# A sorted expert stage in 24 groups instead of 31, sixteen of them of two halves

## The chip, the core and the metric

The kernel runs on one core of one Trainium2 chip. The time is that of the device, in microseconds (us), for one execution of the whole program. A core has five engines with a queue each: TensorE (PE in the profile, with its weight loads as PEld), VectorE (DVE), ScalarE (ACT), GpSimd (POOL) and SyncE (SP), which here only issues DMAs. Engines wait for each other by semaphores. SBUF is the working memory, of 128 partitions; TensorE writes into PSUM.

## The reference, cut to what matters

A decoder layer on 2048 tokens of width 256: a linear recurrence, a cross attention, and a feed-forward part with one shared expert and 16 routed ones, of which each token uses one (K = 1). The change is in the feed-forward part:

```
logits = hidden @ router_w.T
top_vals, top_idx = jax.lax.top_k(logits, K)              # K = 1 of N = 16
scores = sigmoid(top_vals at top_idx, -inf elsewhere)
routed_in = hidden[None, :, :] * scores.T[:, :, None]
gate_up = jnp.einsum('nth,nhf->ntf', routed_in, gate_up_proj)
gate, up = jnp.split(gate_up, 2, axis=-1)
routed_out = jnp.einsum('ntf,nfh->nth', up * silu(gate), down_proj)
shared = silu(hidden @ shared_gate_w.T) * (hidden @ shared_up_w.T) @ shared_down_w.T
x = _layernorm(x + shared + routed_out.sum(axis=0))
```

H and F are 256, the shared width 1024. Everything is float32.

## The kernel before

The program has the stages `before_attention`, `attention`, `route_and_share` and `experts`, each a block in which every engine has its own written-out list of work; a block ends with a barrier of all engines. The change touches the last two.

**Routing and the shared expert** (`route_and_share`). Tokens lie in 16 tiles of 128. The shared expert runs in four chunks of 512 tokens; a chunk has eight steps of hidden columns (`gate_up` on TensorE, `gates` on ScalarE, `hidden` on VectorE), then four tiles of `down`, to which VectorE adds the layer's input in place (`residual`, into `x2`, semaphore `v_base`). While chunk 0 ends, VectorE finds each token's expert (`choose`), and from the counts of two matmuls (`count`) the place of each token in a sorted list (`place`): expert by expert, each expert's rows start at a multiple of 128. The worst case needs 16 + 15 = 31 tiles (`ETILES`). `experts()` of that stage makes the table `te`: tile j belongs to expert te[j]. GpSimd scales each row by its score (`x2s`, eight tiles at a time) and scatters it, with its token number as a 257th column, to `sorted_x` in DRAM by an indirect DMA (line 1068). SyncE had filled `sorted_x` with zeros and the number 2048 (no token) before, and stores the sum of input and shared expert in token order in `routed` (`store_base`, line 1013).

**Experts** (`experts`). One tile j of 128 sorted rows after the other, in a ring of eight:

- SyncE loads `xs` (sorted rows), eight tiles ahead;
- TensorE transposes it (`transpose_x`, L1554), ScalarE copies it to SBUF (L1456), TensorE multiplies by the gate and up weights of expert te[j] (`gate_up`, L1560, 128 x 512 into `bgu`);
- ScalarE makes the silu (L1460), VectorE the product (L1491), TensorE transposes it (`transpose_h`, L1569), VectorE copies (`copy_h`, L1495), TensorE multiplies by the down weights (`down`, L1578, 128 x 256 into `by`);
- VectorE adds the residual row `base` (`whole`, L1507), takes its statistics (L1509, L1512); GpSimd makes the inverse deviation of two tiles at a time (`inverse`, L1419 and L1421), VectorE the shift (L1517), ScalarE normalises (L1465);
- GpSimd gathers `base` from `routed` by the row numbers, two tiles ahead (L1412), and scatters the result to `out` (L1426); rows with number 2048 are skipped.

TensorE's order in slot j is `transpose_x(j+1)`, `transpose_h(j-1)`, `gate_up(j)`, `down(j-1)`; GpSimd's in step j is `gather(j+2)`, with odd j `inverse`, then `store(j-3)`. VectorE's is `copy_h(j-1)`, `product(j)`, `row_number(j+1)`, with odd j `shift`, `whole(j-1)`. The engines run eight slots written out, then hardware loops (`Fori`) of eight, then the rest.

Of the kernel before, what the change touches and what calls it, by code (L numbers as in the profile page):

```python
# [5 lines left out]
F32 = mybir.dt.float32  # L6
# [6 lines left out]
P = 128  # L13
# [882 lines left out]
ETILES = TILES + EXPERTS - 1  # L896
# [7 lines left out]
def route_and_share(nc, io, mem):  # L904
# [9 lines left out]
    with ExitStack() as ctx:  # L914
# [26 lines left out]
        incl = sb("incl", [P, EXPERTS])  # L941
        off = sb("off", [P, 2, EXPERTS])
        posf = sb("posf", [P, TILES])
        cmpj = sb("cmpj", [P, ETILES, EXPERTS])
        tef = sb("tef", [P, 2, ETILES])
# [15 lines left out]
        d_r, d_wd, d_zero, d_scatter = sem("d_r"), sem("d_wd"), sem("d_zero"), sem("d_scatter")  # L961
        g_zero = sem("g_zero")
# [23 lines left out]
        def _(sp):  # L986
# [23 lines left out]

            def store_base(c):
                sp.wait_ge(v_base, (c + 1) * QT)
                sp.dma_start(io["routed"][0:S, :].rearrange("(t p) n -> p t n", p=P)[:, c * QT:(c + 1) * QT, :],
                             x2[:, c * QT:(c + 1) * QT]).then_inc(mem["d_base"], 16)

            for c in range(CHUNKS - 1):
                store_base(c)
# [8 lines left out]
            store_base(CHUNKS - 1)  # L1026

        @block.gpsimd
        def _(pool):
# [21 lines left out]
            for half in range(2):  # L1051
# [59 lines left out]
        def _(dve):  # L1111
# [38 lines left out]

            def place():

                counts = carry[:, TILES, :].unsqueeze(2).to_broadcast([P, EXPERTS, TILES])
                thresholds = grid[:, GRID_THR:GRID_THR + TILES].unsqueeze(1).to_broadcast([P, EXPERTS, TILES])
                step(dve.tensor_tensor(work[:, 0], counts, thresholds, ALU.is_gt))
                step(dve.tensor_reduce(nt[:], work[:, 0], AX.X, ALU.add))
                step(dve.tensor_tensor_scan(incl[:], onesr[:], nt[:], 0.0, ALU.mult, ALU.add))
                step(dve.tensor_tensor(off[:, 0], incl[:], nt[:], ALU.subtract))
                step(dve.tensor_scalar(off[:, 1], off[:, 0], float(P), None, ALU.mult))
                step(dve.tensor_tensor(work[:, 0], bp[:, 0:256].rearrange("p (t n) -> p t n", n=EXPERTS),  # L1160
                                       carry[:, 0:TILES, :], ALU.add))
                step(dve.tensor_tensor(work[:, 1], work[:, 0], by_expert(off[:, 1]), ALU.add))
                step(dve.tensor_tensor(work[:, 0], work[:, 1], oneh[:], ALU.mult))
                step(dve.tensor_reduce(posf[:], work[:, 0], AX.X, ALU.add))
                dve.tensor_copy(pos[:], posf[:]).then_inc(v_pos, 1)

            def experts():

                tiles = grid[:, GRID_J:GRID_J + ETILES].unsqueeze(2).to_broadcast([P, ETILES, EXPERTS])
                step(dve.tensor_tensor(cmpj[:], by_expert(incl[:], ETILES), tiles, ALU.is_le))  # L1170
                step(dve.tensor_reduce(tef[:, 0], cmpj[:], AX.X, ALU.add))
                step(dve.tensor_scalar(tef[:, 1], tef[:, 0], float(EXPERTS - 1), None, ALU.min))
                step(dve.tensor_copy(te[:], tef[:, 1]))
# [54 lines left out]
            count()  # L1228
            place()
            residual(0, (2, 3))  # L1230
            experts()
            with dve.Fori(1, CHUNKS) as c:
                for f in range(FK):
                    hidden(c, f)
                residual(c)
# [93 lines left out]
TURNS = (ETILES - 1) // UNROLL  # L1329

def experts(nc, io, mem):

    te, ident = mem["te"], mem["ident"]
    w_gate_up, w_down = mem["w_gate_up"], mem["w_down"]
    with ExitStack() as ctx:  # L1336
# [30 lines left out]
        g_c4, filler = sem("g_c4"), sem("filler")  # L1367
# [5 lines left out]

        block = ctx.enter_context(nc.Block())

        @block.sync
        def _(sp):
            xs_rows = io["sorted_x"].rearrange("(t p) n -> p t n", p=P)

            def load(j, r):  # L1380
                sp.dma_start(xs[:, r], xs_rows[:, bass.ds(j, 1), :].squeeze(1)).then_inc(d_xs[r], 16)

            with sp.Fori(0, TURNS - 1) as i:
                for r in range(UNROLL):
                    sp.wait_ge(p_x, i * UNROLL + (r + 1))
                    sp.wait_ge(v_row, i * UNROLL + (r + 1))
                    sp.sem_inc(filler, 1)
                    load(i * UNROLL + (r + UNROLL), r)
            for j in range(TURNS * UNROLL, ETILES):
                sp.wait_ge(p_x, j - UNROLL + 1)  # L1390
                sp.wait_ge(v_row, j - UNROLL + 1)
                load(j, j % UNROLL)
            for r in range(UNROLL):
                sp.wait_ge(d_y[r], 16 * ((ETILES - 1 - r) // UNROLL + 1))

        @block.gpsimd
        def _(pool):
# [8 lines left out]
            def gather(j, r, reused):  # L1406
                pool.wait_ge(v_row, j + 1)
                pool.sem_inc(filler, 1)
                if reused:
                    pool.wait_ge(v_y, j - AHEAD + 1)  # L1410
                    pool.sem_inc(filler, 1)
                pool.indirect_dma_start(base[:, r % AHEAD, :], None, io["routed"][0:S, :], bass.IndirectOffsetOnAxis(row[:, r:r + 1], 0),  # L1412
                                        bounds_check=S - 1, oob_is_err=False).then_inc(d_b[r % AHEAD], 16)

            def inverse(m, r, n):

                pair = slice(r, r + n)
                pool.wait_ge(v_mv4, 2 * m + n)
                pool.tensor_tensor(ve4[:, pair], mv4[:, pair, 1], eps4[:, 0:n], ALU.add).then_inc(g_l4, 1)  # L1419
                pool.wait_ge(g_l4, m + 1)  # L1420
                pool.tensor_tensor(rstd4[:, pair], ve4[:, pair], mhalf4[:, 0:n], ALU.pow).then_inc(g_r4, 1)  # L1421

            def store(j, r):
                pool.wait_ge(a_out, j + 1)
                pool.sem_inc(filler, 1)
# [3 lines left out]
            def step(j, n, m):  # L1429

                if not (isinstance(j, int) and j + 2 >= ETILES):
                    gather(j + 2, (n + 2) % UNROLL, not (isinstance(j, int) and j + 2 < AHEAD))
                if n % 2:
                    inverse(m, n - 1, 2)
                if not (isinstance(j, int) and j < 3):
                    store(j - 3, (n - 3) % UNROLL)

            gather(0, 0, False)
            gather(1, 1, False)
            for n in range(UNROLL):  # L1440
                step(n, n, n // 2)
# [252 lines left out]
```

## Time and profile before

| what | us |
|---|---|
| median of 3 runs (lowest, highest) | 941.9 (939.98, 943.53) |
| the profiled execution, its own time | 938.92 |
| its span in the trace | 937.1 |
| PE busy in the span | 891.1 (95%) |
| stage `experts`: first instruction to the end of the span | 820.99 to 937.1 |
| the last `gate_up` of the stage starts | 917.80 |
| the last scatter to `out` starts and ends on GpSimd | 930.75, 931.77 |
| busy in the stretch 826 to 917.8: PE, DVE, ACT, POOL | 90.70, 52.02, 34.09, 67.21 |

The profiled execution is 3.0 us under the median; 1.8 us of its time lie outside its span. A matmul's end in the trace is modelled, and matmuls overlap: the distance from one start to the next says what one costs, not its duration. A busy PE says that something is in its array, not that nothing could be left out.

### The profile page before, as it was taken

To read this page: it belongs to the slowest core of one execution; us is meant where nothing else is said; L and a number is where in the kernel's file an instruction comes from. 1 tells how busy PE (TensorE), PEld (TensorE's weight loads), DVE (VectorE), ACT (ScalarE), POOL (GpSimd) and SP (SyncE) were. 2 spreads that over 40 slices of the span, in tenths; PEclk is the share of its full clock that TensorE was granted. 3 is DMA by queue.
4 is the path that set the end of the run, shared out by engine and by line. 5 is a ranking of instruction groups with operands and counts; after the bars stand their busy time and mean duration, and the time that the engine had idled before them with its cause. 6 is when DMAs were issued, how large, how long until landed. Compare 5 with 4: busy or idle time off the path is not lost. (4 is left out here: it accounts for less than half of the span.)

```text
span 937.1 us, 12963 instructions
## 1 busy us (share of the span) xinstructions
PE 891.1 (95%) x4616; PEld 527.6 (56%) x4616; DVE 551.5 (59%) x1123; ACT 351.8 (38%) x493; POOL 593.3 (63%) x397
## 2 busy tenths in 40 slices
PE   6998799999999999999999999998899999989993
PEld 3655355545555555565554564544678888855551
DVE  2898557667747767757766756754645121145552
ACT  2245144434525544435443434451441121123332
POOL 0454198898878889869889869882114400047785
PEclk9999899999999999999999999999999999999997
DMA  8013300000001000001000001040795100423210
GB/s 277 27 50 111 109 1 1 23 1 1 1 1 45 24 1 1 1 1 46 23 1 0 2 1 45 1 157 1 197 351 193 54 14 22 135 90 111 81 39 15
DMA packets 42873, 52.86 MB, mean 56 GB/s; under 512 B 4400, under 2 KB 33856, under 8 KB 42816
## 3 DMA queue, kind: packets, MB, share of 16 engines
q1 hardware_dynamic: 35808, 44.21, 14.8%
q0 software_dynamic: 3744, 6.32, 2.1%
q10 hardware_dynamic: 3264, 1.57, 0.6%
q8 instruction: 36, 0.59, 0.3%
q14 instruction: 21, 0.17, 0.1%
HBM read 38.42 MB, written 17.59 MB: 60 GB/s over the span
## 5 line engine op out<-in xcount | busy, mean ns | idle before, releaser
L607 POOL TENSOR_TENSOR accG<-accG,probs 128x1024 f32<-128x1024 f32 (+1 forms) x170 | 405.2, 2384 | 38.5 <-ACT probs L630 23.4
L630 ACT ACTIVATE probs<-st 128x1024 f32<-128x1024 f32 (+1 forms) x208 | 212.7, 1026 | 202.9 <-PE st L794 197.3
L674 DVE TENSOR_REDUCE mxp<-mx 128x1 f32<-128x512 f32 x360 | 231.9, 686 | 60.0 <-PE mx L780 54.6
L816 PE MATMUL av<-probs,V 128*64 128x512 f32 (+1 forms) x832 | 191.7, 598 | 0.0
L780 PE MATMUL mx<-K_hi,Q_hi 64*128 64x512 f32 (+1 forms) x480 | 137.9, 380 | 0.0
L816 PEld LDWEIGHTS av<-probs,V 128*64 128x64 f32 (+1 forms) x832 | 55.4, 136 | 105.7 <-issue 83.9
L794 PE MATMUL st<-Q_hi,K_hi 64*128 64x512 f32 (+1 forms) x416 | 113.0, 445 | 0.9 <-ACT probs L630 0.9
L780 PEld LDWEIGHTS mx<-K_hi,Q_hi 64*128 64x128 f32 x480 | 73.8, 184 | 52.0 <-issue 26.8
L794 PE MATMUL st<-M,ones_r 64*128 64x512 f32 (+1 forms) x416 | 101.1, 392 | 0.0
L794 PE MATMUL st<-Q_hi,K_lo 64*128 64x512 f32 (+1 forms) x416 | 96.7, 392 | 0.0
L794 PE MATMUL st<-Q_lo,K_hi 64*128 64x512 f32 (+1 forms) x416 | 94.5, 394 | 0.0
L794 PEld LDWEIGHTS st<-Q_hi,K_hi 64*128 64x128 f32 (+1 forms) x416 | 48.3, 180 | 47.0 <-ACT probs L630 30.5
L689 DVE RECIPROCAL misc<-misc 128x128 f32<-128x128 f32 x64 | 61.4, 960 | 13.5 <-PE misc L833 13.5
L1560 PE MATMUL bgu<-w_gate_up,xsT 128*128 x124 | 58.4, 594 | 1.0 <-ACT xsT L1456 1.0
L1177 DVE TENSOR_TENSOR hT<-hT,bu 128x512 f32<-128x512 f32 x32 | 22.0, 687 | 61.8 <-ACT hT L1090 57.5
L1295 PE MATMUL bt<-wd,hT 128*128 128x256 f32 x256 | 56.3, 380 | 0.4 <-DVE x L1186 0.4
L1090 ACT ACTIVATE hT<-bg 128x512 f32<-128x512 f32 x32 | 19.1, 597 | 99.4 <-PE bu L1280 97.2
L607 POOL TENSOR_TENSOR accG<-probs 128x1024 f32<-128x1024 f32 x16 | 38.3, 2395 | 27.9 <-ACT probs L630 27.9
L794 PEld LDWEIGHTS st<-M,ones_r 64*128 64x128 f32 (+1 forms) x416 | 50.9, 181 | 7.2 <-DVE M L659 0.3
L1295 PEld LDWEIGHTS bt<-wd,hT 128*128 128x128 f32 x256 | 48.5, 190 | 7.4 <-DVE x L1186 0.8
L1398 POOL MEMSET mhalf<- 128x2 f32 x1 | 0.1, 99 | 82.9 <-POOLq L914 82.9
L794 PEld LDWEIGHTS st<-Q_lo,K_hi 64*128 64x128 f32 (+1 forms) x416 | 49.6, 182 | 3.7
(198 smaller groups left out, 1238.0 us busy)
## 6 DMA issues: line engine op xcount, KB each, us to landing
w_gate_up<-in_gate_up SPq DMA_DIRECT2D x4, 2048.0 KB, 20.1
w_down<-in_down SPq DMA_DIRECT2D x2, 2048.0 KB, 15.8
xs<-scratch_sorted_x SPq DMA_DIRECT2D x31, 128.5 KB
scratch_sorted_x<-zero SPq DMA_DIRECT2D x7, 514.0 KB, 8.3
xT<-in_xT SPq DMA_DIRECT2D x4, 512.0 KB, 6.7
xring<-in_x SPq DMA_DIRECT2D x4, 512.0 KB, 8.7
scratch_x1b<-xT SPq DMA_DIRECT2D x4, 512.0 KB, 2.9
x<-scratch_x1b SPq DMA_DIRECT2D x4, 512.0 KB, 4.3
```

The costliest lines, as they stand in the source:

```text
L607: pool.tensor_tensor(total[0:r], so_far[0:r], probs[0:r, place(S, t)], ALU.add).then_inc(g_add, 1)
L630: act.activation(probs[0:r, place(S, t)], st[g % 2][0:r, :], ACT.Exp, scale=DH ** -0.5).then_inc(a_probs, 1)
L674: dve.tensor_reduce(mxp[:, F % 2, h * QT + i, j:j + 1], mx[h][:, 0:kn], AX.X, ALU.max).then_inc(v_mx, 1)
L689: dve.reciprocal(misc[:, cols], misc[:, cols]).then_inc(v_rsum, 1)
L780: mm = pe.matmul(mx[h][:, a * kn:(a + 1) * kn], Q_hi[F % 2][rows, q * P:(q + 1) * P], K_hi[rows, F % PAIRS, k0:k0 + kn], start=True, stop= ...
L794: mm = pe.matmul(st[g % 2][0:r, h * QC:(h + 1) * QC], w, q, start=(part == 0), stop=(part == MAXIMA))
L816: mm = pe.matmul(av[h * DH:(h + 1) * DH, :], V[0:r, t, (2 * p + h) * DH:(2 * p + h + 1) * DH], probs[0:r, place(S, t), h * QC:(h + 1) * QC ...
L1090: act.activation(hT[:, f], bg[f % 2][:], ACT.Silu).then_inc(a_silu, 1)
L1177: dve.tensor_tensor(hT[:, f], hT[:, f], bu[f % 2][:], ALU.mult).then_inc(v_h, 1)
L1295: mm = pe.matmul(bt[i % 2][:, 0:D], hT[:, f, i * P:(i + 1) * P], wd[:, f, :], start=(f == 0), stop=(f == FK - 1))
L1398: pool.memset(mhalf4[:], -0.5).then_inc(g_c4, 1)
L1560: mm = pe.matmul(bgu[r % 2][:], xsT[:, r, k * P:(k + 1) * P], w_gate_up[:, bass.ds(e * DK + k, 1), :].squeeze(1), start=(k == 0), stop=(k ...
```

## The change

The sorted list gets another layout of 24 groups of 128 rows. An expert with n rows fills ceil(n/128) - 1 whole tiles first ("pairs" in the code: two halves of 64); these go to groups 0 to 7, of which each has one expert, from `te` (`WHOLE` = 8). The remaining 1 to 128 rows of expert e are its rest: the first 64 of them go to the second half of group 8 + e, whose expert is fixed; rows past 64 of a rest ("odd") go to the first half of one of the groups 8 to 23, with an expert from `te`. If whole tiles are more than eight, the further ones take first halves too (`over`, `BEYOND`, `spread`). So groups 8 to 23 are computed with two experts' weights: each matmul with 128 columns of stationary rows becomes two with 64, which write to the PSUM partitions 0 to 63 and 64 to 127 (`products`). All 24 groups are always computed.

The residual rows are sorted too. In place of `store_base` and of GpSimd's gathers, GpSimd scatters each finished tile of `x2` to a second DRAM list `sorted_base` (`scratch_base`), twelve tiles in the routing stage and four at the start of the expert stage; SyncE fills that list with zeros before, and in the expert stage loads `base` with plain DMAs, four groups ahead, after `d_base` has counted all 16 scatters. The loops of the expert stage are written out for 24 groups, `te` is read once per slot instead of twice, and GpSimd's order becomes `store`, `store`, `inverse`. ScalarE normalises two groups together. VectorE's routing work grows and is put between the steps of the shared expert's chunk 1.

```diff
-ETILES = TILES + EXPERTS - 1
+HALF = P // 2
+WHOLE = TILES // 2
+ETILES = WHOLE + EXPERTS
...
-            for c in range(CHUNKS - 1):
-                store_base(c)
+            for t in range(0, ETILES, ZT):
+                n = min(ZT, ETILES - t)
+                sp.dma_start(mem["sorted_base"].rearrange("(t p) n -> p t n", p=P)[:, t:t + n, :],
+                             zero[:, 0:D].unsqueeze(1).to_broadcast([P, n, D])
+                             ).then_inc(d_bzero, 16)
...
-            store_base(CHUNKS - 1)
...
+            pool.wait_ge(d_bzero, 16 * ((ETILES + ZT - 1) // ZT))
+            for t in range(TILES - QT):
+                pool.wait_ge(v_base, t + 1)
+                pool.indirect_dma_start(mem["sorted_base"][:, :], bass.IndirectOffsetOnAxis(pos[:, t:t + 1], 0),
+                                        x2[:, t], None).then_inc(mem["d_base"], 16)
...
             count()
+            per_expert()
+            residual(0, (2, 3))
+            hidden(1, 0)
+            offsets()
+            hidden(1, 1)
+            past_pairs()
+            hidden(1, 2)
             place()
-            residual(0, (2, 3))
+            hidden(1, 3)
+            spread()
+            hidden(1, 4)
+            experts_at()
+            hidden(1, 5)
             experts()
...
+            def load_base(j):
+                at_least(sp, v_y, j - AHEAD + 1)
+                sp.dma_start(base[:, j % AHEAD], base_rows[:, j, :]).then_inc(d_b[j % AHEAD], 16)
+
+            sp.wait_ge(mem["d_base"], 16 * TILES)
+            for j in range(AHEAD):
+                load_base(j)
+            for j in range(UNROLL, ETILES + AHEAD):
+                if j < ETILES:
+                    load(j)
+                load_base(j - AHEAD)
...
-            pool.memset(base[:, :, :], 0.0).then_inc(g_c4, 1)
-            pool.wait_ge(g_c4, 3)
-            pool.wait_ge(mem["d_base"], 16 * CHUNKS)
...
+            for tile in range(TILES - QT, TILES):
+                pool.indirect_dma_start(mem["sorted_base"][:, :], bass.IndirectOffsetOnAxis(pos[:, tile:tile + 1], 0),
+                                        x2[:, tile], None).then_inc(mem["d_base"], 16)
...
+            inverse(0)
+            for m in range(1, ETILES // 2):
+                store(2 * m - 2)
+                store(2 * m - 1)
+                inverse(m)
+            store(ETILES - 2)
+            store(ETILES - 1)
...
+            def products(out, cols, rows_T, j, chosen, weights):
+
+                for k in range(DK):
+                    chosen_rows = weights[:, bass.ds(chosen * DK + k, 1), :].squeeze(1)
+                    if j < WHOLE:
+                        mm = pe.matmul(out[:, 0:cols], rows_T[:, k * P:(k + 1) * P], chosen_rows, start=(k == 0), stop=(k == DK - 1))
+                    else:
+                        own = (j - WHOLE) * DK + k
+                        pe.matmul(out[0:HALF, 0:cols], rows_T[:, k * P:k * P + HALF], chosen_rows, start=(k == 0), stop=(k == DK - 1))
+                        mm = pe.matmul(out[HALF:P, 0:cols], rows_T[:, k * P + HALF:(k + 1) * P], weights[:, own, :],
+                                       start=(k == 0), stop=(k == DK - 1))
+                return mm
```

**TensorE, one slot of the expert stage.** Before, from the second `gate_up` matmul (k = 1) of a tile to the first `down` matmul of the tile before it; ISA and TENSOR_LOAD rows are register work and the read of `te`:

```order
L1560 ISA
L1560 MATMUL bgu<-w_gate_up,xsT 128x512
L1547 TENSOR_LOAD te
L1547 ISA x2
L1578 ISA [waits v_y,v_hT]
L1578 MATMUL by<-w_down,hTt 128x256
```

The same piece of a slot of the groups 8 to 23 in the changed kernel:

```order
L1598 ISA
L1598 MATMUL bgu<-w_gate_up,xsT 64x512
L1599 MATMUL bgu<-w_gate_up,xsT 64x512
L1598 ISA [waits v_y,v_hT]
L1598 MATMUL by<-w_down,hTt 64x256
L1599 MATMUL by<-w_down,hTt 64x256
```

Each matmul of 128 rows has become two of 64 with the same number of streamed columns, and the second read of the table is gone. The transposes around this piece stay at 128 x 128.

**GpSimd, the start of the expert stage.** Before, from the stage's first instruction (L1412 gathers residual rows, L1419 and L1421 are `inverse`, L1426 scatters the output):

```order
L1398 MEMSET mhalf 128x2
L1400 MEMSET eps 128x2 [waits g_c4]
L1402 MEMSET base 128x1024 [waits g_c4]
L1412 DMA base<-scratch_routed,row 128x256 [waits v_row,g_c4,d_base]
L1412 DMA base<-scratch_routed,row 128x256 [waits v_row] x3
L1419 TENSOR_TENSOR ve<-mv,eps 128x2 [waits v_mv4]
L1421 TENSOR_TENSOR rstd<-ve,mhalf 128x2 [waits g_l4]
L1412 DMA base<-scratch_routed,row 128x256 [waits v_row,v_y] x2
```

The changed kernel, from the same place (L1486 scatters the last four residual tiles, L1500 the output):

```order
L1481 MEMSET mhalf 128x2
L1483 MEMSET eps 128x2 [waits g_c4]
L1486 DMA scratch_base<-x_49,pos 3072x256 [waits g_c4]
L1486 DMA scratch_base<-x_49,pos 3072x256 x3
L1493 TENSOR_TENSOR ve<-mv,eps 128x2 [waits v_mv4]
L1495 TENSOR_TENSOR rstd<-ve,mhalf 128x2 [waits g_l4]
L1500 DMA out<-ysb,row 2048x256 [waits a_out] x2
```

The gathers are gone, four scatters stand before everything else, and two output scatters stand between one `inverse` and the next.

**VectorE, from the counts to the shared expert's chunk 1.** In the changed kernel (L1239 is `hidden`, L1248 `residual`; the tables `per_...` and `off_...`, one number per expert, are new):

```order
L1170 TENSOR_TENSOR over<-over 128x1 [waits v_route]
L1171 TENSOR_SCALAR per_odd_to<-per_odd_to,over 128x16 [waits v_route]
L1248 TENSOR_TENSOR x_49<-bt,x_49 128x256 [waits p_dn,g_x2s,v_route]
L1248 TENSOR_TENSOR x_49<-bt,x_49 128x256 [waits p_dn]
L1239 TENSOR_TENSOR hT<-hT,bu 128x512 [waits a_silu]
L1175 TENSOR_TENSOR off_pair<-per_pairs_to,per_pairs 128x16
L1176 TENSOR_SCALAR off_pair<-off_pair 128x16 [waits v_route]
L1177 TENSOR_TENSOR off_rest<-grid,per_paired 128x16 [waits v_route]
```

Before, ten instructions from the comparison with the thresholds to the cast of `pos` stood between the counts and this `residual`, and four more behind it; now eleven stand before it and 39 behind it, in six lots, each behind one `hidden` of chunk 1, the cast of `pos` in the fourth.

## Rows read from the trace of the kernel before

**Rows 1.** The page: busy time, share and instructions of TensorE.

```profile
PE 891.1 (95%) x4616; PEld 527.6 (56%) x4616; DVE 551.5 (59%) x1123; ACT 351.8 (38%) x493; POOL 593.3 (63%) x397
```

**Rows 2.** A stretch's busy time: start:end, length, engines (records), PEclk, DMA share, GB/s.

```profile
826.00:917.80 91.80, 90.70 (x347) 53.79 (x346) 52.02 (x184) 34.09 (x83) 67.21 (x81) 1.00 0.26 74
```

**Rows 3.** Chain of work that ended last, one slot: start, us, what.

```profile
826.04 1.72 PE bgu L1560 x4
827.76 0.86 PE by L1578 x4
828.62 0.22 PE bx L1554 x2
828.84 0.29 PE bh L1569 x2
829.12 1.72 PE bgu L1560 x4
```

**Rows 4.** Timeline of TensorE in attention: start, us, engine, instruction.

```profile
509.05 1.08 PE L816 MATMUL av<-probs,V 128*64 128x512 f32 x4
510.06 0.50 PE L780 MATMUL mx<-K_hi,Q_hi 64*128 64x512 f32 x2
510.49 2.80 PE L816 MATMUL av<-probs,V 128*64 128x512 f32 x12
513.22 0.33 PE L749 MATMUL mx<-ident,nm 128*128 128x128 f32 x1
```

**Rows 5.** Timeline at the end of the routing counts, VectorE.

```profile
707.97 0.42 DVE L1155 TENSOR_TENSOR work<-carry,grid 128x256 f32<-128x256 f32 x1
709.11 0.18 DVE L1158 TENSOR_TENSOR off<-incl,nt 128x16 f32<-128x16 f32 x1
717.84 0.69 DVE L1177 TENSOR_TENSOR hT<-hT,bu 128x512 f32<-128x512 f32 x1 [2.09 <-issue]
```

**Rows 6.** Timeline of GpSimd, the last of eight scatters and the wait behind it.

```profile
720.94 0.96 POOL L1068 DMA_INDIRECT scratch_sorted_x<-x2s,pos  x1 [0.30 <-issue]
723.99 3.66 POOL L1058 TENSOR_SCALAR x2s<-x,esc 128x256 f32<-128x256 f32 x8 [2.09 <-DMA scratch_sorted_x<-x2s,pos]
```

**Rows 7.** Timeline at the start of the expert stage.

```profile
821.15 0.10 POOL L1400 MEMSET eps<- 128x2 f32 x1
828.66 0.42 DVE L1507 TENSOR_TENSOR ysb<-by,base 128x256 f32<-128x256 f32 x1
829.79 0.39 DVE L1495 COPY hTt<-bh 128x256 f32<-128x256 f32 x1
```

**Rows 8.** Timeline in the expert stage, the way from silu to the next down product.

```profile
901.21 0.38 ACT L1460 ACTIVATE sil<-bgu 128x256 f32<-128x256 f32 x1 [1.62 <-PE bgu L1560]
904.51 0.72 POOL L1421 TENSOR_TENSOR rstd<-ve,mhalf 128x2 f32<-128x2 f32 x1
905.26 0.16 DVE L1517 SCALAR_TENSOR_TENSOR shift<-mv,rstd 128x2 f32<-128x2 f32 x1
906.49 0.39 DVE L1495 COPY hTt<-bh 128x256 f32<-128x256 f32 x1
907.18 1.03 PE L1578 MATMUL by<-w_down,hTt 128*128 x4
```

**Rows 9.** Timeline of the last tile.

```profile
917.80 1.88 PE L1560 MATMUL bgu<-w_gate_up,xsT 128*128 x4
919.72 0.38 ACT L1460 ACTIVATE sil<-bgu 128x256 f32<-128x256 f32 x1 [2.21 <-PE bgu L1560]
922.46 1.13 PE L1578 MATMUL by<-w_down,hTt 128*128 x4 [1.41 <-DVE hTt L1495]
927.18 0.97 POOL L1426 DMA_INDIRECT out<-ysb,row  x1 [0.31 <-issue]
928.46 0.57 POOL L1421 TENSOR_TENSOR rstd<-ve,mhalf 128x1 f32<-128x1 f32 x1
930.75 1.02 POOL L1426 DMA_INDIRECT out<-ysb,row  x1 [1.71 <-ACT ysb L1465]
```

More of the change, by code:

```diff
@@ L1335, in experts @@
     w_gate_up, w_down = mem["w_gate_up"], mem["w_down"]
+    x2, pos = mem["x2"], mem["pos"]
     with ExitStack() as ctx:
@@ L1468, in slot @@
-            def slot(j, n, m):
-                if not (isinstance(j, int) and j == ETILES - 1):
-                    copy_x(j + 1, (n + 1) % UNROLL)
-                gate(j, n)
-                if not (isinstance(j, int) and j < 4):
-                    normalise(j - 4, (n - 4) % UNROLL, m - 2)
-            copy_x(0, 0)
-            for n in range(UNROLL):
-                slot(n, n, n // 2)
-            with act.Fori(1, TURNS) as i:
-                for n in range(UNROLL):
-                    slot(i * UNROLL + n, n, i * (UNROLL // 2) + n // 2)
@@ L1487, in _, with product @@
+            copy_x(0)
+            for j in range(ETILES):
+                if j + 1 < ETILES:
+                    copy_x(j + 1)
+                gate(j)
+                if j >= 4 and j % 2 == 0:
+                    normalise(j // 2 - 2)
+            normalise(ETILES // 2 - 2)
+            normalise(ETILES // 2 - 1)
         @block.vector
         def _(dve):
-            def product(j, r):
+            def product(j):
                 dve.wait_ge(a_s, j + 1)
-                dve.tensor_tensor(h[:, r], sil[:, r], bgu[r % 2][:, FE:2 * FE], ALU.mult).then_inc(v_hh, 1)
@@ L1546, in expert_of @@
             def expert_of(j):
[L1547 to L1554 removed]
+                return pe.value_load(te[0:1, j:j + 1], min_val=0, max_val=EXPERTS - 1)
@@ L1570, in transpose_h, with down @@
                 mm.then_inc(p_h, 1)
-            def down(j, r):
-                e = expert_of(j)
+            def down(j, chosen):
                 pe.wait_ge(v_hT, j + 1)
-                if not (isinstance(j, int) and j < 2):
-                    pe.wait_ge(v_y, j - 1)
-                for k in range(DK):
-                    mm = pe.matmul(by[r % 2][:, 0:D], hTt[:, r, k * P:(k + 1) * P],
-                                   w_down[:, bass.ds(e * DK + k, 1), :].squeeze(1), start=(k == 0), stop=(k == DK - 1))
-                mm.then_inc(p_y, 1)
@@ L1595, in _ @@
[L1595 to L1604 removed]
+                at_least(pe, v_y, j - 1)
@@ new lines, in down @@
+                products(by[j % 2], D, hTt[:, ring(j)], j, chosen, w_down).then_inc(p_y, 1)
+            transpose_x(0)
+            transpose_x(1)
+            pe.wait_ge(mem["d_experts"], 16 * (EXPERTS // 4 + 2))
+            chosen = expert_of(0)
+            gate_up(0, chosen)
+            for j in range(1, ETILES):
+                before, chosen = chosen, expert_of(j)
+                if j + 1 < ETILES:
+                    transpose_x(j + 1)
+                transpose_h(j - 1)
+                gate_up(j, chosen)
+                down(j - 1, before)
@@ L1607, in program @@
+            transpose_h(ETILES - 1)
+            down(ETILES - 1, chosen)
 def program(nc, io, stages=3):
```

292 lines of the change are left out of this document (136 added, 156 removed).

## The prediction

> **What bounds the kernel now.** First the page: TensorE is busy 95% of the span [rows 1], so work taken from the other engines is worth nothing unless TensorE waits for it. Then the stage that changes, by the table of stretches: from 826 to 917.8 TensorE is busy 90.70 of 91.80 us, at a granted clock of 1.00 (the 2.4 GHz level), while GpSimd, the next, has 67.21 [rows 2]. Then the chain of waits inside it: one slot is 1.72 (gate and up) + 0.86 (down) + 0.22 + 0.29 (the two transposes) = 3.09 us, all of it TensorE [rows 3]. So the stage costs 3.09 us for each tile, full or nearly empty, and the number of tiles is what to look at. The gate-up of tile 1 starts at 826.04 [rows 3], that of tile 30 at 917.80 [rows 9]: 29 slots in 91.76 us, which is 2.1 us more than 29 x 3.09 = 89.6. Behind it comes a tail of 937.1 - 917.80 = 19.3 us, which the chain gives mostly to GpSimd and to DMAs landing.
>
> **Fewer groups.** From the gate-up of group 1 to that of group 23 there are 22 slots. If each cost 3.09 us, that would be 68.0 us instead of 91.76: **-23.8 us**. This takes the 2.1 us of small stalls as gone too. They may belong to the hardware loops, which go, or to the waits among engines, which stay; I keep half of their share for 22 slots (1.6 us): **+0.8 us**, ends 0 and 1.6.
>
> **Two halves instead of one matmul.** A split group issues twice the matmuls, with the same number of streamed columns each. Whether that doubles the time is read in attention, where the value product is written in the same way: two 64-column matmuls into the two halves of the PSUM partitions. There four records take 510.06 - 509.05 = 1.01 us to the next start, and twelve take 513.22 - 510.49 = 2.73 [rows 4]. So a record more costs (2.73 - 1.01) / 8 = 0.215 us, half of the 1.72 / 4 = 0.43 us of a full-width record of the same 512 columns [rows 3]: the two halves run side by side. Eight records of a split gate-up are 8 x 0.215 = 1.72 us, as before, and down keeps its 0.86 in the same way. What is left is the change of shape. The same rows give 1.01 - 4 x 0.215 = 0.15 us as the fixed part of a burst. The way in from a 128 x 128 transpose no row shows; between nothing and a whole record of delay (0.43), I take 0.05, near the fixed part's own size. So a split slot costs 0.20 us more, with ends 0.05 (the fixed part mostly hidden) and 0.58. Slots 8 to 22 are 15: **+3.0 us**, ends 0.8 and 8.7. The second read of `te` goes as well; the chain shows no wait for it, so nothing.
>
> The trace shows a fixed part of 0.15 us a burst. On this the Trainium skill, "TensorEngine Tiling (Array Packing)", section Tiling Modes, says that going from one tiling mode to another drains TensorE. By that rule each split slot pays twice, on the way in and out, and the section Single matmul latency of "TensorE: Matmul & The Clock Gate" gives 166 ns for what a matmul alone can't hide; an estimate from that page is 0.33 us per slot, 5.0 us in place of my 3.0. The rows show one such price and not the second; the second is rival 1.
>
> **The residual rows at the start.** GpSimd's clear of `base` (L1402) and its gathers go. In their place it scatters four tiles of `x2`. After the two memsets, at 821.25 [rows 7], four scatters of 0.96 us with 0.30 between them [rows 6] are over near 826.2; the landing of the last of such a row took 2.09 us [rows 6]: 828.3. Only then may SyncE load the first residual rows. No row shows how long 128 KB take to land; between 0.5 and 4 us I take 2.7 with issue, so that `whole(0)` starts near 831.0 instead of 828.66 [rows 7]. It is not `whole(0)` that matters but what is queued behind it on VectorE: `copy_h(1)`, which starts 1.13 us after it [rows 7] and takes 0.39, for which `down(1)` waits. That copy would be over at 832.5; `down(1)` started at 827.76 + 3.09 = 830.84 [rows 3]: **+1.7 us**, once, ends 0 and 3.5. Later loads are issued four groups ahead, over 12 us early, and are hidden.
>
> **GpSimd's order.** That the gathers go brings nothing by itself, since GpSimd was not the bound. But `inverse` now stands behind two stores. The silu of an even group starts at 901.21 [rows 8], the two normalisations behind it would end near 902.1 and 902.6 (an estimate, at half a microsecond each), the stores take 0.97 with 0.31 between [rows 9], so GpSimd comes to `inverse` near 904.6 and is through at about 905.6. The shift on VectorE stood at 905.26 and the down product at 907.18, with the copy it needs over at 906.88 [rows 8]: 0.3 us of slack, 0.1 to 0.2 short. In split slots the 0.20 us more per slot cover that; for the three pairs among whole groups **+0.4 us**, ends 0 and 3.
>
> **The tail.** Counted from the last silu (T = 919.72 [rows 9]): the last down product started at T + 2.74, because `whole` of the tile before stood ahead of the copy it needs. The change puts the copy first: T + 1.8, statistics over near T + 4.2. GpSimd had its last inverse at 928.46 = T + 8.7 [rows 9], behind its backlog of gathers and stores; now the stores of groups 20 and 21 are over by T + 3.4, and the power starts at T + 4.5. From there to the first scatter it was 2.29 us (928.46 to 930.75 [rows 9]), and there are two scatters of 0.97 with 0.31 between: the last ends at T + 9.1 instead of T + 12.05. That is -3.0, with 0.2 given back for the last split group: **-2.8 us**, ends -4 and -1.
>
> **Routing: nothing.** VectorE has 11 instructions before the residual instead of 10, two of them of 0.42 and nine of 0.18 us [rows 5], each with some 0.04 of wait: 2.8 us where 3.6 stood. The other 39 come in six lots, each behind a `hidden` step, before which VectorE sat idle 2.09 us [rows 5]. The longest (10 x 0.22, 5 x 0.46) are 2.2 and 2.3 us, so a step is at most 0.3 us late, and TensorE needs it only a whole step (some 2.6 us) later. `pos` comes 15 us later, near 726.5. The 16 + 12 scatters with their waits then last to about 785, when chunk 2's residual is there; cover to the barrier at 821: 36 us. Were this cover gone, each scatter more would cost 1.27. Zeroing 3.1 MB more is off the path. Ends -0.5 and +1.
>
> **Sum.** -23.8 + 0.8 + 3.0 + 1.7 + 0.4 - 2.8 = -20.7 us. Against the profiled execution, 938.92, that is 918.2; the median of the runs lies 3.0 higher, so 941.9 - 20.7 = **921.2 us**.
>
> **Rivals.**
> 1. *The change of shape is dear.* Each split slot waits for the array to empty on both sides, and the first weights are loaded with nothing to hide them: near the end 0.58 instead of 0.20 per slot. For it: no row shows the way in. Against it: the burst of four costs only 0.15. It gives 15 x 0.38 = 5.7 more: 927.
> 2. *A new wait takes the place of the work.* GpSimd's two stores before `inverse` hold the shift, VectorE's in-order queue holds the copy, and TensorE waits 0.5 us in each of 11 pairs (5.5 instead of 0.4). For it: the slack is 0.3 us [rows 8]. Against it: it has no more gathers. 926; with a late first residual (3.5) 928.
> 3. *The halves run one after the other*, because here both have their own weights from the stream side and a register address. Then a split group costs 1.72 + 0.86 = 2.58 us more, 16 of them 41.3: 941.9 - 20.7 - 3.2 + 41.3 = 959, slower. It decides from 23.9 / 16 = 1.5 us per split group on. Against it: rows 4 show a pair, also with two different streams, at half price.
> 4. *The gain is not seen,* since a slot is held by the way gate-up, silu, product, transpose (0.2 us of slack) and the seven groups were cheaper than 3.09. Rows 3 speak against it: unchanged.
>
> **Chances.** My forecast 0.68, rival 1 0.14, rival 2 0.11, rival 3 0.05, rival 4 0.02. The forecast's own range is 916 to 925. Low end for the whole: split slots at 0.05, no late start and no stalls: 941.9 - 26 = 916, with a microsecond for the measurement 915. High end: rivals 1 and 2 partly together, 932; what is left out above is rival 3 and the worst of both. The shown runs spread by 3.6 us, so 0.5% (4.7 us) is about what can be told from no change: faster by more 0.93, within it 0.02, slower 0.05.
>
> **What would show it.** In the changed profile: 24 slots, of 3.09 us for the groups to 7 and near 3.3 from 8 on; the records of a split gate-up at a spacing of 0.215. If the spacing is 0.43, rival 3 holds; if a gap stands before the first record behind `transpose_h`, rival 1; if `down` waits for `hTt` and VectorE's shift for `rstd`, rival 2. `whole(0)` some 10 us behind the stage's first instruction would confirm the late start; under 8, refute it. The last output scatter should end 9 us behind the last silu. The routing stage should end within 1 us of 821. The forecast is wrong if a split slot is over 3.7 us or under 3.1.

## The result and the profile after

The changed kernel took 927.24 us (median of 4 runs, 926.6 to 927.5) against 942.12 before (4 runs), a ratio of 0.9855, 95% interval 0.9837 to 0.9873. The forecast was 921.2. Run again later it took 917.90 (917.33 to 919.14) against 939.88, a ratio of 0.9769 (0.9751 to 0.9788). Both times lie in the whole range, 915 to 932. But 927.24 lies outside the forecast's own range, 916 to 925, and near the prices of rivals 1 and 2 (927 and 926), by coincidence: the two times differ by a stall of 8 us and by 2.3 us at a lower granted clock. The stall was seen again on one chip and not on two others; which chip gave the first result is not on record. First the profile of the 927 run (its own time 927.47, span 925.6).

TensorE's row of the page, beside [rows 1]: 44 instructions more, 11.8 us less busy.

```profile
PE 879.3 (95%) x4660; PEld 511.6 (55%) x4660; DVE 547.3 (59%) x1113; ACT 343.7 (37%) x472; POOL 564.6 (61%) x366
```

The stretch from the gate-up of group 1 to that of group 23, then two of the routing stage (columns as in [rows 2]):

```profile
835.49:910.33 74.84, 72.75 (x381) 34.57 (x379) 40.08 (x140) 25.83 (x63) 28.36 (x39) 1.00 0.33 99
640.00:660.00 20.00, 17.03 (x72) 8.76 (x71) 10.63 (x15) 3.18 (x4) 2.49 (x2) 0.88 0.00 1
660.00:680.00 20.00, 19.04 (x78) 14.09 (x79) 12.65 (x36) 11.05 (x27) 2.66 (x9) 0.78 0.89 207
```

The stretch is 74.84 us where the 29 slots of [rows 2] took 91.76. TensorE is still its bound, but now waits 2.1 us in it, and GpSimd is busy 28.36 us instead of 67.21.

The chain of waits (start, us, what; short steps left out) from the late first residual, by a wait for GpSimd, to a split slot, beside [rows 3]:

```profile
831.95 0.97 POOL scratch_base L1486
835.78 2.40 DMA scratch_base<-x,pos
838.20 1.88 DMA base<-scratch_base
840.18 0.44 DVE ysb L1557
841.20 0.40 DVE hTt L1545
841.74 1.13 PE by L1595 x4
...
851.25 0.99 POOL out L1500
852.54 0.73 POOL rstd L1495
853.38 0.44 DVE ysb L1557
854.48 0.32 DVE hTt L1545
854.94 1.12 PE by L1595 x4
...
862.95 0.57 PE bgu L1598
863.53 0.42 PE bgu L1598
863.96 0.42 PE bgu L1598
864.39 0.42 PE bgu L1598
864.82 0.21 PE by L1598
...
865.68 0.37 PE bx L1608 x2
866.05 0.22 PE bh L1619 x2
866.27 0.57 PE bgu L1598
```

Three things are to be seen. A split slot is 866.27 - 862.95 = 3.32 us, against 3.09 for a whole one. The first residual comes late: `whole(0)` starts at 840.18, 8.9 us after the stage's first instruction (831.25). And the chain passes from GpSimd's store over `rstd` (the inverse deviation, which `inverse` makes) to `hTt` and down: the way of rival 2. The records of TensorE (start, us, engine) show the halves of a split product side by side:

```profile
862.88 0.64 PE L1598 MATMUL bgu<-w_gate_up,xsT 128*64 x1
862.89 0.64 PE L1599 MATMUL bgu<-w_gate_up,xsT 128*64 128x512 f32 x1
```

The wait table (us in total, times, longest) of the expert stage:

```profile
DVE shift L1566 <- POOL rstd L1495: 9.1, 11, 2.1
PE by L1595 <- DVE hTt L1545: 1.9, 2, 1.3
DVE ysb L1557 <- DMA base<-scratch_base: 1.9, 1, 1.9
PE by L1598 <- DVE hTt L1545: 1.0, 1, 1.0
```

VectorE waits for `rstd` in all 11 pairs; the copy behind it makes TensorE wait too. The tail, beside [rows 9]:

```profile
912.31 0.38 ACT L1519 ACTIVATE sil<-bgu 128x256 f32<-128x256 f32 x1 [2.00 <-PE bgu L1599]
916.93 0.98 POOL L1500 DMA_INDIRECT out<-ysb,row  x1 [0.31 <-issue]
918.21 0.72 POOL L1495 TENSOR_TENSOR rstd<-ve,mhalf 128x2 f32<-128x2 f32 x1
921.90 0.98 POOL L1500 DMA_INDIRECT out<-ysb,row  x1 [0.30 <-issue]
```

The expert stage as a whole took 925.6 - 831.25 = 94.35 us against 937.1 - 820.99 = 116.1: **-21.8**, forecast -20.7. But it began 10.3 us later than before, and for that nothing was forecast. Some 2.3 us of it were lost before VectorE or GpSimd ran any changed code: in the stretches from 640 to 660 and to 680 the granted clock was 0.88 and 0.78, where the changed kernel run again shows 1.00 and 0.91. That is not the change: the kernel before with a run of sixteen scatters, told below, has the old code up to there and shows 0.86 and 0.79, and its stage begins at 822.51. The other 8.0 lie in chunk 2 of the shared expert, whose first silu is at 752.98 and that of chunk 3 at 797.12: 44.1 us where before there were 36.0. The timeline there (in brackets: idle time before, and what ended it):

```profile
756.61 0.60 ACT L1096 ACTIVATE hT<-bg 128x512 f32<-128x512 f32 x1 [3.04 <-PE bu L1356]
764.39 0.97 POOL L1074 DMA_INDIRECT scratch_base<-x,pos  x1 [0.30 <-issue]
765.78 0.60 ACT L1096 ACTIVATE hT<-bg 128x512 f32<-128x512 f32 x1 [8.57 <-remote]
766.41 0.69 DVE L1239 TENSOR_TENSOR hT<-hT,bu 128x512 f32<-128x512 f32 x1 [8.48 <-issue]
767.15 0.80 PE L1356 MATMUL bg<-x2T,wgate_high 128*128 x1 [5.85 <-issue]
768.00 0.60 ACT L1096 ACTIVATE hT<-bg 128x512 f32<-128x512 f32 x1 [1.62 <-remote]
```

ScalarE should start a silu every 2.79 us; it starts none between 756.61 and 765.78, though its product was ready. VectorE and TensorE then stand still behind it, and the matmuls that follow take 0.63 instead of 0.40 us: the granted clock is 0.50 from 769 to 771, the 1.2 GHz level, after TensorE sat idle for 5.85 us. GpSimd issues sixteen scatters back to back from 745.21, the last of them ends at 765.36, and 0.42 us later ScalarE goes on (in the other profiles with the stall it goes on 1.3 to 2.7 us behind the last scatter).

### The profile page after: what moved, and what is told of

Read it like the earlier page. It is cut to its first block and busy times, and to the rows that moved or that the text cites. A ratio compares the mean times of both kernels' runs of the same rounds, so it can differ in the third digit from the quotient of the medians.

```text
span 925.6 us, 12487 instructions
## 1 busy us (share of the span) xinstructions
PE 879.3 (95%) x4660; PEld 511.6 (55%) x4660; DVE 547.3 (59%) x1113; ACT 343.7 (37%) x472; POOL 564.6 (61%) x366
## 5 line engine op out<-in xcount | busy, mean ns | idle before, releaser
L1239 DVE TENSOR_TENSOR hT<-hT,bu 128x512 f32<-128x512 f32 x32 | 22.0, 687 | 61.7 <-ACT hT L1096 47.1
L794 PEld LDWEIGHTS st<-Q_hi,K_lo 64*128 64x128 f32 (+1 forms) x416 | 47.6, 181 | 6.5
L1500 POOL DMA_INDIRECT out<-ysb,row x24 | 24.1, 1004 | 42.4 <-ACT ysb L1524 38.7
```

Source lines behind the costliest of these rows:

```text
L794: mm = pe.matmul(st[g % 2][0:r, h * QC:(h + 1) * QC], w, q, start=(part == 0), stop=(part == MAXIMA))
L1239: dve.tensor_tensor(hT[:, f], hT[:, f], bu[f % 2][:], ALU.mult).then_inc(v_h, 1)
L1500: pool.indirect_dma_start(io["out"][:, :], bass.IndirectOffsetOnAxis(row[:, r:r + 1], 0), ysb[:, r, :], None, bounds_check=S - 1, oob_is_e ...
```

## Experiments

The twelve runs fell on three chips, each with the kernel before beside them. It took 940.22 us on the first chip, 938.43 on the second and 939.88 on the third.

### Where the stall comes from

**The residual scatters moved behind chunk 2** (first chip):

```diff
             pool.wait_ge(d_bzero, ...)
+            pool.wait_ge(v_base, TILES - QT)
             for t in range(TILES - QT):
-                pool.wait_ge(v_base, t + 1)
```

> The changed kernel, with its twelve residual scatters of the routing stage all held back until chunk 2's residual is there (some 795 us), so that the burst of 16 scatters without a pause (745.2 to 765.4) becomes one of 8, and another of 12 runs in chunk 3. In the changed kernel ScalarE's silu of chunk 2 starts at 765.78, 7.2 us late, just when the last scatter of the burst is over (765.36). Theory S (a long run of GpSimd scatters holds ScalarE up): chunk 2 is clean, and either nothing is late (the burst of 12 in chunk 3 is too short: 927.2 - 8 = 919 us) or a stall of the same kind comes in chunk 3, 5 to 8 us (924 to 927). Theory V (VectorE's chunk 1 being written out, or its later `pos`, shifts something, and the scatters are bystanders): the stall stays at chunk 2, 927 us.

Measured: 923.32 us (921.46 to 926.1), 0.981. Chunk 2 takes 36.1 us again, with one silu 0.75 us late (756.69) beside its run of eight, and the stall has moved to chunk 3, under the twelve scatters that now stand there in one run from 787.77:

```profile
794.83 0.60 ACT L1096 ACTIVATE hT<-bg 128x512 f32<-128x512 f32 x1 [2.19 <-PE bu L1356]
799.16 0.60 ACT L1096 ACTIVATE hT<-bg 128x512 f32<-128x512 f32 x1 [3.73 <-remote]
804.88 1.08 ACT L1096 ACTIVATE hT<-bg 128x512 f32<-128x512 f32 x2 [5.13 <-PE bu L1356]
```

It costs 5.7 us there (789.26 to the stage's start at 829.56 is 40.3; before, 34.6). So on this chip the stall goes where the run of scatters goes; VectorE's routing code, which stayed where it was, is not its cause.

**ScalarE's chunks 1 to 3 written out, without the hardware loop** (first chip):

```diff
...
-            with act.Fori(1, CHUNKS) as c:
-                gates(c)
+            for c in range(1, CHUNKS):
+                gates(c, False)
```

> The changed kernel, with ScalarE's list of the shared expert's chunks 1 to 3 written out, with constant waits, instead of a hardware loop. Theory L (ScalarE's loop, with its register work and its jump, is what the burst of scatters holds up; VectorE and TensorE are only behind it): no stall at 757 to 766, about 919 us. Theory S without L (the scatters hold ScalarE whatever its code): the stall stays, 927 us.

Measured: 926.52 us (925.7 to 926.98), 0.9849. The stall stays: silus at 754.75 and then 764.69, with 9.34 us of idle ended by "remote", and chunk 2 takes 45.5 us (750.40 to 795.94). The loop on ScalarE is not its cause.

**A pause between the eighth and the ninth scatter of the run** (second chip, and again on the third):

```diff
             pool.wait_ge(d_bzero, ...)
+            pool.wait_ge(d_scatter, 16 * TILES)
             for t in range(TILES - QT):
```

> The changed kernel with one wait more: GpSimd lets its sixteen scatters of the sorted rows land before it issues the first of the residual rows, so that the unbroken run of sixteen becomes two of eight with a pause of about 2 us (the landing of the last). Theory 1, what holds the other engines up is the length of the unbroken run (the hold-up began at the ninth or tenth scatter of it, whether the run was of sixteen or of twelve): with runs of eight it is gone, chunk 2 of the shared expert takes 36 to 37 us instead of 44.1, time 918 to 921. Theory 2, it is the number of scatters in some 20 us, and a pause of 2 us is too short to matter: chunk 2 stays at 43 to 45, time 926 to 928. Theory 3, it is the scatters into the residual scratch themselves (zeroed just before, rows of another width), not their number: the stall stays too, but starts within the first three of the second eight.

Measured: 918.33 us (917.61 to 918.86), 0.9792 (0.9768 to 0.9816). No silu is late. That looked like theory 1, but another kernel on the same chip takes that reading away: it has the sixteen in one run, and no silu is late there either.

**The kernel before with a run of sixteen scatters** (second chip):

```diff
-            sp.wait_ge(d_scatter, 16 * TILES)
+            sp.wait_ge(d_scatter, 16 * (TILES + TILES // 2))
...
+            for n in range(TILES // 2):
+                t = TILES // 2 + n
+                pool.indirect_dma_start(mem["spare"][:, :], ...pos[:, t:t + 1]..., x2s[:, n, :], None
+                                        ).then_inc(d_scatter, 16)
```

> The kernel before, with eight scatters more of the rows of its second half, into memory that nobody reads, right behind its second eight: an unbroken run of sixteen on GpSimd in an otherwise unchanged kernel. The last eight repeat data that is there already; the output is that of the kernel before. Theory 1 (an unbroken run of more than eight or nine scatters holds the other engines up): the shared expert's chunk in which they fall takes 7 to 9 us more, time 947 to 951. Theory 3 (the scatters of the residual rows or what else the change put there is needed): 940 to 942.

Measured: 939.63 us (938.6 to 941.64), 1.0015 (1.0 to 1.0029). The sixteen run from 729.88 to 750.0 without a break. But this run could not show the stall: the ninth scatter starts at 740.14, and no silu is due between 735.36 and 751.95, when TensorE does the down products of the chunk:

```profile
735.36 0.60 ACT L1094 ACTIVATE hT<-bg 128x512 f32<-128x512 f32 x1 [2.17 <-PE bu L1284]
751.95 0.60 ACT L1094 ACTIVATE hT<-bg 128x512 f32<-128x512 f32 x1 [14.69 <-PE bu L1284]
```

It shows only that the down products are not held (the next chunk's first silu comes 16.6 us behind the last one, as in every kernel here). What decides is the kernel of all whole groups with `rstd` first (told below). It has the changed kernel's code up to the expert stage, with sixteen scatters back to back from 743.14, and its silus too are on time, at 756.65, 759.44, 762.22. Twelve and sixteen scatters had stalled each of four kernels on the first chip. What differed was the chip, or the hour, so the changed kernel itself was still wanted as a control.

**The changed kernel again** (third chip), no edit.

> The changed kernel itself, once more. The kernel of all whole groups with rstd first ran sixteen scatters back to back on the second chip with no silu late, and the same code up to the expert stage had lost 8 us to them on the first chip. So either the stall belongs to the chip, and is here only if this is a chip of that kind: then this kernel takes 926 to 928 with it and 918 to 920 without; or it comes and goes with something in the kernels that no reading of the code shows: then it is here whatever the chip.

Measured: 917.90 us (917.33 to 919.14), 0.9769 (0.9751 to 0.9788), the same code as the 927.24. Sixteen scatters run from 742.78 to 762.9, and the silus beside them:

```profile
756.26 0.60 ACT L1096 ACTIVATE hT<-bg 128x512 f32<-128x512 f32 x1 [2.19 <-PE bu L1356]
759.04 0.60 ACT L1096 ACTIVATE hT<-bg 128x512 f32<-128x512 f32 x1 [2.19 <-PE bu L1356]
761.83 0.60 ACT L1096 ACTIVATE hT<-bg 128x512 f32<-128x512 f32 x1 [2.19 <-PE bu L1356]
```

Its expert stage starts at 820.92, where that of the kernel before started at 820.99, and lasts 94.8 us. Neither the stall nor the 2.3 us of lower clock is there.

**The pause again** (same edit, third chip):

> The kernel with a pause of about 2 us between the eighth and the ninth scatter of the run of sixteen, once more, beside the changed kernel on the same chip. If the changed kernel stalls here: 918 to 921 if the length of the unbroken run is what matters, 925 to 928 if not. If the changed kernel does not stall here: the same as it within 1 us.

Measured: 918.82 us (917.74 to 920.14), 0.978. Within 1 us of the changed kernel; with no stall to cure, the pause buys nothing.

**The kernel before with the run of sixteen again** (third chip):

> The kernel before with a run of sixteen scatters, once more, beside the changed kernel on the same chip. If the changed kernel stalls here and this one too (947 to 951), the run of scatters alone is enough; if the changed kernel stalls and this one does not (939 to 943), the run needs something else that the change brought. If the changed kernel does not stall, neither does this one.

Measured: 939.11 us (937.75 to 940.71), 0.9994 (0.9982 to 1.0006). No stall here either, but again its ninth to sixteenth scatters (738.72 to 748.6) lie between two silus (734.49 and 751.10), so it adds nothing.

What follows: on the first chip the stall went with a long run of scatters (it followed them from chunk 2 to chunk 3), and it needs something besides that the first chip had and the two others hadn't: there a run of sixteen with silus beside it lost nothing, in one kernel on each. Whether that is the chip itself or a condition of it at that hour isn't told apart; nor is it known which engine's fetch or semaphore is held, since "remote" and "issue" name none. Whether a pause or pacing cures it where it occurs was not tried: the two kernels that have one ran on chips without it.

### What the expert stage's parts cost

**`rstd` ahead of the two stores** (first chip):

```diff
-            for m in range(1, ETILES // 2):
+            for m in range(1, ETILES // 2 - 1):
+                inverse(m)
                 store(2 * m - 2)
                 store(2 * m - 1)
-                inverse(m)
+            store(ETILES - 4)
+            store(ETILES - 3)
+            inverse(ETILES // 2 - 1)
```

> The changed kernel, with GpSimd's inverse put before the two stores in each pair but the last, which is the order nearer to the kernel before. In the changed kernel VectorE's shift waits 9.1 us in all for the inverse, and every second or fourth slot is 0.25 us longer than 3.32. If the stores ahead of the inverse cost what the prediction's rival 2 says in part: the longer slots go, some 1 to 2.5 us less, 925 to 926 us. If the longer slots have another cause: 927.2, no change. The 8 us stall in routing stays in both.

Measured: 924.95 us (924.1 to 925.84), 0.9831, with the stall still in it; its expert stage is 92.0 us where the changed kernel's was 94.35. Its routing stage lost 0.7 us more, so the stages are compared and not the times: 2.4 us. Of VectorE's 9.1 us of waiting for `rstd` 1.7 are left, in one place. Rival 2's way was real, at half of its price.

**All 24 groups multiplied as whole groups**, first in the old order (first chip), then with `rstd` first (second chip). The second halves of groups 8 to 23 are multiplied by another expert's weights; what the fixed experts should do with them is left out:

```diff
-                    if j < WHOLE:
+                    if j < ETILES:
```

> The changed kernel, with all 24 groups multiplied as whole groups of 128 rows by one expert (the second halves of groups 8 to 23 get the wrong weights: that part of the computation is left out). It measures what the change of shape costs: the split slots stand at 3.32 to 3.59 us in the trace, the whole ones at 3.09. By the prediction's term (0.20 us per split slot, 16 of them) 3.2 us less, 924.0; by the trace (mean 3.39, 0.30 more) 4.8 us less, 922.4; if splitting is free, 927.2.

> The changed kernel with rstd ahead of the stores as in the kernel of that experiment (924.95), and all 24 groups multiplied as whole groups of 128 rows, so that the second halves of groups 8 to 23 get another expert's weights: the outputs of those rows are left out. With all groups whole but the old order the stage was 1.6 us shorter than the changed kernel's and waited for the copy of h for 5 us. If the split shape costs about 0.23 a slot and the old order had swallowed part of it, this stage is 92.0 - 16 x 0.23 = 88.3, time about 921 to 922. If the split costs nothing of itself, it stays at 92.0, time 924.5 to 925.5.

Measured: 926.5 us (925.56 to 928.18), stage 92.7; and 911.92 us (911.49 to 912.97), 0.9728, stage 909.8 - 821.32 = 88.5. In the old order the shorter slots are given back in part: TensorE waits 5.0 us, 7 times, for the copy `hTt`. With `rstd` first nothing is given back (so the order costs 92.7 - 88.5 = 4.2 us where all groups are whole), and the price of the split shape can be read against the next kernel, which ran beside it.

**Residual scatters paced, and `rstd` first** (second chip; third again):

```diff
             for t in range(TILES - QT):
-                pool.wait_ge(v_base, t + 1)
+                if t < 6:
+                    pool.wait_ge(v_h, 2 * FK + 2 + t)
+                pool.wait_ge(v_base, t + 3 if t in (6, 7) else t + 1)
...
```

> The changed kernel with two edits. The first six residual scatters wait each for one more hidden step of chunk 2 of the shared expert (2.79 us apart), the seventh and eighth for its first two residual rows; and in the expert stage each pair's rstd goes ahead of the two stores of the pair before. If the stall is the unbroken run of scatters and nothing else, chunk 2 takes 36.1 (stall of 8.0 gone) and chunk 3 34.6 as before; with the 2.3 us that the order alone gave, the time is 927.2 - 8.0 - 2.3 = 917, and 916 to 919 covers it. If the stall comes from scatters that meet the hidden steps at all, however spaced, it is 921 to 925, with silus late by some tenths at each of eight steps.

> The kernel with paced residual scatters and rstd ahead of the stores, once more, beside the changed kernel on the same chip. If the changed kernel stalls here: 916 to 919, about 10 us less than it. If it does not: 2 to 3 us less than it, which is the order of rstd and stores alone.

Measured: 915.75 us (915.13 to 916.27), 0.9763 (0.9739 to 0.9787); again 916.35 (914.71 to 917.09), 0.9743 (0.9724 to 0.9762), beside 917.90 of the changed kernel (0.9769). It is faster than the changed kernel: no run of it was as slow as the fastest of that one (917.33). Since that one did not stall there, the order of `rstd` and stores is the difference: 1.5 us in the time, and 2.6 against the kernel with the pause on the second chip. The stages say 94.7 - 92.1 = 2.6 us on the second chip and 94.8 - 92.0 = 2.8 on the third; the 1.5 is less because this kernel's profile there has the low clock from 640 to 680 (0.89 and 0.77) and begins its stage at 823.30, 2.4 us later. Its silus of groups 8, 9 and 23:

```profile
852.08 0.38 ACT L1524 ACTIVATE sil<-bgu 128x256 f32<-128x256 f32 x1 [1.78 <-PE bgu L1604]
855.44 0.38 ACT L1524 ACTIVATE sil<-bgu 128x256 f32<-128x256 f32 x1 [1.71 <-PE bgu L1604]
...
901.83 0.38 ACT L1524 ACTIVATE sil<-bgu 128x256 f32<-128x256 f32 x1 [1.89 <-PE bgu L1604]
```

and those of the kernel of whole groups:

```profile
850.74 0.38 ACT L1522 ACTIVATE sil<-bgu 128x256 f32<-128x256 f32 x1 [1.62 <-PE bgu L1598]
853.82 0.39 ACT L1522 ACTIVATE sil<-bgu 128x256 f32<-128x256 f32 x1 [1.45 <-PE bgu L1598]
...
897.04 0.38 ACT L1522 ACTIVATE sil<-bgu 128x256 f32<-128x256 f32 x1 [1.73 <-PE bgu L1598]
```

From group 8 to 23 that is 49.75 us against 46.30: (49.75 - 46.30) / 15 = 0.23 us for each split slot, and 915.75 - 911.92 = 3.8 us in the time.

## Why the prediction was right, and where its sizes were off

**Fewer groups, -23.8: right.** Whole slots are 3.09 us, as before [rows 3], and the count did the rest. The 0.8 us kept for stalls of unknown origin was too much: before, every slot longer than 3.09 us (3.25 to 3.68) lies between the silus of tiles 6 and 21, one in each pair, and the last nine are at 3.09; whether the loops or a wait among the engines made them is not shown. Now, with `rstd` first the whole groups 3 to 6 stand at 3.08 to 3.09 and nothing more (their silus are at 836.49 and 845.74, three slots).

**Split shape, +3.0: right.** Measured 0.23 us a slot, 3.5 for 15, against 0.20. The halves run side by side, so rival 3 falls, and the price is far from rival 1's 0.58. In the chain the first pair of a gate-up takes 0.57 instead of 0.42 (+0.15, the fixed part read from [rows 4]), and the transposes behind a split down take 0.37 instead of 0.22 where they follow at once: a price on both sides. So the size came near for a reason that was only half right: the term held 0.15 for one side and 0.05 for the other; measured are 0.15 on both, of which 0.07 comes back, since the second pair of transposes takes 0.22 instead of 0.29. The Trainium skill, "TensorEngine Tiling (Array Packing)", section Tiling Modes, says that a change of mode drains the array: the two places agree with it. The estimate of 0.33 us a slot from the Trainium skill, "TensorE: Matmul & The Clock Gate", section Single matmul latency, was too high by 0.1.

**Late first residual, +1.7: right.** `whole(0)` was expected about 10 us behind the stage's start and came 8.9 behind (9.2 on the third chip). The 2.7 us taken for the load, which no row of before showed, measured 2.0: the scatters had landed at 838.18. On the third chip the silus of groups 2 and 3 are 835.10 - 830.17 = 4.93 us apart instead of 3.09: +1.8; in the first profile 845.08 - 840.49 = 4.59: +1.5.

**GpSimd's order, +0.4: too small.** It costs 2.4 to 2.8 us by the stages: 1.9 in the slots (from the silu of group 3 to that of group 23 it is 67.23 us, and 65.34 with `rstd` first), the rest in the tail. The working expected 0.1 to 0.2 us for each pair among whole groups, and that in split slots the 0.20 us more cover it. Neither holds: the silus of groups 6 and 7, still whole, are 858.26 - 854.34 = 3.92 us apart (+0.8), and from there every fourth slot takes 3.59 instead of 3.32. By the chain the two stores wait for a normalisation, that for the shift behind the previous `rstd`, and the next `rstd` for the two stores, so that a late pair can make the next one late. Rival 2's mechanism happened, inside the range that the term had (0 to 3).

**Tail, -2.8: too small, by two errors of opposite sign.** The last scatter ends at 922.88, 10.6 us behind the last silu (912.31), not 9.1: the stores of the pair before were over at T + 5.6, not T + 3.4. Half of that is again GpSimd's order: with `rstd` first the last scatter ends 9.8 us behind. That is 1.5 less than before instead of 3.0. But from the last scatter's end to the end of the span it is 2.7 us now and was 5.3 (931.77 [rows 9] to 937.1); no engine works in either. The whole tail is 13.3 against 17.4 us. Why the end of the program is 2.6 us shorter I didn't test, and that it makes up for the 1.5 is luck.

**Start of the stage, 0 forecast: -0.8.** From its first instruction to the gate-up of group 1 it is 835.49 - 831.25 = 4.2 us, and was 5.05 (826.04 [rows 3] less 820.99). The first gate-up waits 0.39 us for the first copy of `xsT`, 1.04 before.

**Routing, 0 (-0.5 to +1): right without the stall and the low clock, 8 us wrong with the stall.** VectorE's 39 instructions cost nothing: the stage began at 820.92 to 821.77 in four profiles on the second and third chip (at 822.38 and 823.30 in the two with the lowest clock from 640 to 680). The step that failed is this sentence: "The 16 + 12 scatters with their waits then last to about 785 ... cover to the barrier". It asked only whether the scatters end in time, not what their length of run does to the other engines. The trace of before gave a hint that I passed over: beside the burst of eight the silus kept 2.77 us except one, at 723.22, that was 0.46 us late (none is late beside such a burst on the second and third chip). No rival carried this, and the interval of this term, up to +1, was too narrow; the total range held only because the others were wide.

Taken together, without the stall and the clock: forecast -20.7, on the third chip 917.90 - 939.88 = **-22.0**. The measured terms add up to -23.8 + 3.5 + 1.7 + 1.9 - 4.1 - 0.8 = -21.6, and the stage shows -21.8 and, run again, -21.3. That the sum is within 1 us is in part luck: the split shape and GpSimd's order in the slots came out 2.0 us dearer than forecast, the stalls, the tail and the start 2.9 us cheaper.

## What to carry to other kernels

When a stage costs the same for each tile, full or empty, count the tiles first; packing two half tiles side by side costs 0.23 us a slot here against 3.09 for each slot it saves. When an in-order queue holds both the stores of one pair and the small operation that the next pair needs, put the small one first; a slack of tenths is used up by pairs that hand their lateness on. And run a change on more than one chip before explaining a difference of 1%: here two of three chips didn't have the stall. And when a load is added to provoke a stall, see that it lies beside the instructions that it could hold up: here the old kernel's longer run of scatters fell where no silu was due.

## What the hardware showed that was not expected

- On the first chip, and in the first result, a run of twelve or sixteen indirect scatters from GpSimd, 1.27 us apart, held ScalarE up with its input ready, and VectorE and TensorE behind it; the shared expert's chunk took 5.7 us longer with twelve and 9.4 to 10.7 with sixteen (8.1 in the first result), and up to 10.0 us lay between two silus (755.62 and 765.58 in the kernel of whole groups in the old order). It began near the eighth to tenth scatter of a run and ended 0.4 to 2.7 us behind the last. On two other chips the same code lost nothing.
- After such a stop (TensorE idle for 5.85 us) matmuls took 0.63 us instead of 0.40, at the 1.2 GHz level, until 771.
- The kernel before differs by 1.8 us between the three chips (938.43 to 940.22; 942.12 beside the first result), the changed one by 9.3 between its two measurements.
- The granted clock from 640 to 680 differs between profiles whose code is the same up to there, on one chip too, and what follows moves with it: 1.00 and 0.91, with the expert stage's start at 820.92, against 0.89 and 0.77, with 823.30, both on the third chip.
